# Making h for two batches at once in 64x32 tiles: one fused AdaLN/FFN kernel on Trainium2

## The reference, cut to what matters

```
# x: (8, 512, 2048); each batch b has its own adapter itok[b], rank 16
Bx    = einsum('bni,bri->bnr', x, cond_B[itok])      # 8 x 512 x 16
y     = einsum('bnr,bor->bno', Bx, cond_A[itok])     # never formed
base  = einsum('bsi,oi->bso', y, base_w) + base_b
res   = einsum('bsi,ri->bsr', y, ffn_A)              # 64 wide
p     = softmax(einsum('bsi,ei->bse', y, router_w))  # 16 experts
comb  = top-2 of p, normalised to sum 1, as a dense (b, s, 16)
delta = einsum('bse,bsr,eor->bso', comb, res, ffn_B)
out   = x + base + 0.5 * delta
```

## Time and profile before

| | |
|---|---|
| median of 3 runs | 458.0 us (456.47 to 458.59) |
| profiled execution | 457.73 us, of it the span of the trace 455.9 us |
| PE busy | 412.8 us, 91% |
| DVE busy | 312.6 us, 69% |
| ACT busy | 107.5 us, 24% |
| POOL busy | 40.4 us, 9% |
| DMA | 135.31 MB, mean 297 GB/s |
| mean granted TensorE clock | 0.992 of full |

### The profile page before, as it was taken

One profiled execution on the slowest core, in us unless ns is written; L12 is line 12 of the kernel. 1 busy time (PEld: TensorE's weight loads), 2 busy tenths in 40 slices (PEclk: granted clock), 3 DMA queues, 4 the chain that ended last, 5 costly groups with the idle time before them and its releaser, 6 DMA issues.

```text
span 455.9 us, 6139 instructions
## 1 busy us (share of the span) xinstructions
PE 412.8 (91%) x2240; PEld 275.2 (60%) x2240; DVE 312.6 (69%) x702; ACT 107.5 (24%) x163; POOL 40.4 (9%) x53
## 2 busy tenths in 40 slices
PE   0587998699888999999999999999999999999996
PEld 0466886466555675566556556655675566566675
DVE  3699799968447657766767775677667766757353
ACT  0002025244553240132023102401220132123110
POOL 4020000001100120012002101200120012002000
PEclk9998999999999999999999999999999999999999
DMA  8999999999999997999889888989998998555845
GB/s 228 363 337 335 340 377 345 336 235 352 269 318 256 346 326 265 289 344 309 286 287 384 323 271 282 365 266 291 330 329 287 290 359 313 188 196 197 312 160 186
DMA packets 89360, 135.31 MB, mean 297 GB/s; under 512 B 5506, under 2 KB 43442, under 8 KB 89330
## 3 DMA queue, kind: packets, MB, share of 16 engines
q1 hardware_dynamic: 63168, 102.08, 67.3%
q10 hardware_dynamic: 26162, 32.84, 23.9%
HBM read 99.23 MB, written 35.65 MB: 296 GB/s over the span
## 4 chain that ended last, share of the span: by engine, by line
PE 69%; DVE 13%; DMA 9%; ACTq 3%; ACT 3%; issue 2%; DVEq 0%
PE ps L874 13%; PE ps L895 12%; PE ps L896 10%; PE ps L897 10%; PE ps L908 7%; PE ps L898 5%; DMA xbuf<-in_L_ffn_base_w 5%; DMA early_u<-in_L_ffn_B 5%; PE ps L839 4%; PE ps L829 4%; DVE xT L707 3%; DVE h_r L688 3%; DVE early L640 3%; ACT bexpT L476 2%; ACTq L281 2%
## 5 line engine op out<-in xcount | busy, mean ns | idle before, releaser
L817 DVE TENSOR_TENSOR xbuf<-ps,xbuf 128x512 f32<-128x512 f32 x128 | 87.0, 679 | 109.9 <-PE ps L898 109.8
L895 PE MATMUL ps<-h_r,u_r 128*128 128x512 f32 x256 | 109.3, 427 | 7.1 <-DVE xbuf L817 7.1
L896 PE MATMUL ps<-h_r,u_r 128*128 128x512 f32 x256 | 100.2, 392 | 0.0
L897 PE MATMUL ps<-h_r,u_r 128*128 128x512 f32 x256 | 100.1, 391 | 0.0
L839 PE MATMUL ps<-early 128*128 128x256 f32 x256 | 65.4, 408 | 20.3 <-DVE early L640 20.3
L895 PEld LDWEIGHTS ps<-h_r,u_r 128*128 128x128 f32 x256 | 48.0, 188 | 47.6 <-issue 20.1
L707 DVE STREAM_TRANSPOSE xT<-xbuf 128x512 f32<-128x512 f32 x112 | 72.0, 681 | 0.0
L640 DVE STREAM_TRANSPOSE early<-xbuf 128x256 f32<-128x256 f32 x128 | 65.9, 584 | 5.2 <-issue 3.7
L839 PEld LDWEIGHTS ps<-early 128*128 128x128 f32 x256 | 49.4, 203 | 32.5 <-issue 16.0
L874 PE MATMUL ps<-bexpT,cur 128*32 128x512 f32 x512 | 61.6, 598 | 2.2 <-DVE h_r L688 1.5
L476 ACT ACTIVATE h_r<-ps 128x512 fp32r<-128x512 f32 x64 | 35.7, 594 | 86.6 <-issue 53.8
(11 more groups left out here) (67 smaller groups left out, 206.3 us busy)
## 6 DMA issues: line engine op xcount, KB each, us to landing
out<-xbuf SPq DMA_DIRECT2D x31, 1024.0 KB, 7.1
xbuf<-in_x SPq DMA_DIRECT2D x28, 1024.0 KB, 7.1
xbuf<-in_x ACTq DMA_DIRECT2D x32, 512.0 KB, 9.6
xbuf<-in_x SPq DMA_DIRECT2D x32, 512.0 KB, 8.5
xbuf<-in_L_ffn_base_w SPq DMA_DIRECT2D x16, 512.0 KB, 18.8
xbuf<-in_L_ffn_base_w ACTq DMA_DIRECT2D x16, 512.0 KB, 19.5
gm_r<-g_hilo SPq DMA_DIRECT2D x128, 32.0 KB, 6.4
early_u<-in_L_ffn_B SPq DMA_DIRECT2D x10, 256.0 KB, 17.3
```

What stands on the lines that cost most here:

```text
L817: dve.tensor_tensor(xs, ps[:, ACC + t % 2, :], xs, ALU.add).then_inc(s_out, 1)
L895: pe.matmul(acc, u_r[:, b.q, 0, h, tok_t], hi, start=(h == 0), stop=False)
L896: pe.matmul(acc, u_r[:, b.q, 0, h, tok_t], lo, start=False, stop=False)
L897: pe.matmul(acc, u_r[:, b.q, 1, h, tok_t], hi, start=False, stop=False)
```

## The change

Batches are grouped as 0, (1, 2), (3, 4), (5, 6), 7. A unit is one chunk c of one batch (four tiles); within a pair the units alternate: chunk 0 of both batches, chunk 1 of both, and so on.

h is made per group in rounds (h_round). One round is eight matmuls in tiles of 64 rows by 32 columns: the upper and lower 64 rows (one expert each) go to two PSUM banks, HB and HB+1, and the 32 weight columns are two batches x 16 (a new table, pairs; for a single batch the other 16 are another batch's or zero). For each batch ACT copies bank HB times a 0/1 mask into a new buffer hm (h_masked) and DVE adds bank HB+1 times the other mask (h_merge). h_hi then rounds from hm on ACT, and the low part of h is subtracted on POOL (h_lo); the low part of u moves from POOL to DVE (u_lo). In a pair the two rounds of a chunk stand before tiles 1 and 3 of the first batch's unit, in a single batch before tiles 0 and 1.

The fronts are placed anew (fronts_at): beside the 16 tiles of batch 0 the fronts of batches 1 and 2, two steps per tile; beside the pair (1, 2) those of 3 and 4; beside (3, 4) those of 5 and 6; beside (5, 6) that of 7, one step for every two tiles; beside batch 7 none. From tile 8 on, tiles use four PSUM banks in place of two. tmp, sbx_r and the loads of g are doubled or rearranged for pairs; cur is gone. The order of the experts in the odd place of a pair is swapped to match.

```diff
+        members = [(0,)] + [(b, b + 1) for b in range(1, NB - 1, 2)] + [(NB - 1,)]
+        units, firsts = [], []
+        for group, batches in enumerate(members):
+            firsts.append(len(units))
+            for c in range(OC):
+                for b in batches:
+                    units.append(Unit(len(units), group, c, b))
+        firsts.append(len(units))
...
+        def rounds_at(u):
+
+            i = h_sets.index((u.group, u.c)) + 1
+            pair = len(members[u.group]) == 2
+            if i == len(h_sets) or pair and u.b != members[u.group][0]:
+                return {}
+            return {1: (i, 0), 3: (i, 1)} if pair else {0: (i, 0), 1: (i, 1)}
+
+        def split_at(u):
+
+            return 0 if len(members[u.group]) == 2 else 1
+
+        def fronts_at(u, t):
+
+            m = (u.index - firsts[u.group]) * NT + t
+            if u.group == 0:
+                f, ms = 1 + m // 8, (m % 8 * 2, m % 8 * 2 + 1)
+            elif u.group == NG - 2:
+                f, ms = NB - 1, (m // 2,) if m % 2 == 0 else ()
+            elif u.group == NG - 1:
+                return []
+            else:
+                f, ms = 2 * u.group + 1 + m // MT, (m % MT,)
+            return [(Front(f), k) for k in ms]
...
-        H_AFTER = 122
+        H_AFTER = (114, 124)
+        HT_AT, HM_AT = 118, 120
...
+        XQUAD_AT = {0: ((1, 0), (1, 1)), 2: ((2, 0), (2, 1))}
+        for group in range(1, NG - 2):
+            for i, at in enumerate((0, 1, 4, 5)):
+                XQUAD_AT[firsts[group] + at] = ((2 * group + 1 + i // 2, i % 2),)
...
+        U_AT = {firsts[b // 2]: b for b in range(2, NB, 2)}
+        U_AT.update({firsts[b // 2 + 1] - 1: b for b in range(3, NB, 2)})
...
+        def tile_bank(n):
+
+            return (ACC, ACC + 1)[n % 2] if n < WIDE_FROM else (ACC, ACC + 1, EB, EB + 1)[n % 4]
...
+            def unit(u):
+                for f, g in XQUAD_AT.get(u.index, ()):
+                    xquad_free(sp, Front(f), g)
+                    load_xquad(sp, f + 1, g, range(0, NQ // 2))
+                cols = slice(u.c * BANK, (u.c + 1) * BANK)
+                slot = slice(u.slot * BANK, (u.slot + 1) * BANK)
+                if u.index == len(units) - 1:
+                    for t in range(NT):
+                        sp.wait_ge(s_out, u.index * NT + t + 1)
+                        sp.dma_start(out_v[u.b, :, t, cols], xres[:, t, slot]).then_inc(s_store[u.slot], 16)
+                    return
+                sp.wait_ge(s_out, (u.index + 1) * NT)
+                sp.dma_start(out_v[u.b, :, :, cols], xres[:, :, slot]).then_inc(s_store[u.slot], 16)
+                if u.b == members[u.group][-1] and u.group + 1 < NG:
+                    load_gm(u.group + 1, u.c)
+                if u.index > 0 and u.index + NC - 1 < len(units):
+                    reload(units[u.index - 1], units[u.index + NC - 1])
+
+            def reload(done, new):
...
+            def h_lo(index):
+
                 for h in range(2):
-                    pool.wait_ge(s_uhi, f.n * 2 + h + 1)
-                    pool.tensor_tensor(u_r[:, f.q, 1, h, :], tmp[:, h, :], f32(u_r[:, f.q, 0, h, :]),
-                                       ALU.subtract).then_inc(s_ulo, 1)
+                    pool.wait_ge(s_hhi, 2 * index + h + 1)
+                    pool.tensor_tensor(h_r[:, index % 2, 1, h, :], hm[:, index % 2, h, :],
+                                       f32(h_r[:, index % 2, 0, h, :]), ALU.subtract).then_inc(s_hlo, 1)
+                pool.wait_ge(s_hlo, 2 * index + 2)
...
-            def h_hi(b, c):
+            def h_masked(i, h):
+
+                group, c = h_sets[i]
+                act.wait_ge(s_h, 2 * i + h + 1)
+                for place in range(len(members[group])):
+                    index = firsts[group] + c * len(members[group]) + place
+                    need(act, s_hlo, 2 * (index - 2) + h + 1 if index > 1 else 0)
+                    act.activation(hm[:, index % 2, h, :], ps[:, HB, :], ACT.Copy,
+                                   scale=mask[:, place:place + 1])\
+                       .then_inc(s_ht, 1)
...
+            def h_hi(index):
+
+                u = units[index]
+                i = h_sets.index((u.group, u.c))
+                count = len(members[u.group])
                 for h in range(2):
-                    act.wait_ge(s_h, (b.n * OC + c) * 2 + h + 1)
+                    act.wait_ge(s_hm, merges[i] + h * count + members[u.group].index(u.b) + 1)
                     if h == 0:
-                        need(act, s_acc, (b.n * OC + c - 1) * NT)
-                    copy(h_r[:, c % 2, 0, h, :], ps[:, HB + h, :]).then_inc(s_hhi, 1)
+                        need(act, s_acc, (index - 1) * NT)
+                    copy(h_r[:, index % 2, 0, h, :], hm[:, index % 2, h, :]).then_inc(s_hhi, 1)
+
+            def u_hi(f, h):
+
+                act.wait_ge(s_up, f.n * 2 + h + 1)
+                copy(u_r[:, f.q, 0, h, :], tmp[:, f.q, h, :]).then_inc(s_uhi, 1)
...
+                    if t == 0 and u.index in U_AT:
+                        act.wait_ge(s_acc, tiles_before(u.index))
+                        for h in range(2):
+                            u_hi(Front(U_AT[u.index]), h)
+                    if t in rounds:
+                        h_masked(*rounds[t])
+                    if t == split_at(u) and u.index + 1 < len(units):
+                        h_hi(u.index + 1)
+                    if u.index * NT + t in E_LATE:
+                        copy_experts(E_LATE[u.index * NT + t])
+                    for f, m in fronts_at(u, t):
+                        slot(f, m)
...
-            def h_lo(b, c):
+            def h_merge(i, h):
+
+                group, c = h_sets[i]
+                count = len(members[group])
+                for place in range(count):
+                    index = firsts[group] + c * count + place
+                    dve.wait_ge(s_ht, merges[i] + h * count + place + 1)
+                    dve.scalar_tensor_tensor(out=hm[:, index % 2, h, :], in0=ps[:, HB + 1, :],
+                                             scalar=mask[:, 1 - place:2 - place], in1=hm[:, index % 2, h, :], op0=ALU.mult,
+                                             op1=ALU.add).then_inc(s_hm, 1)
+
+            def u_lo(f):
+
                 for h in range(2):
-                    dve.wait_ge(s_hhi, (b.n * OC + c) * 2 + h + 1)
-                    dve.tensor_tensor(h_r[:, c % 2, 1, h, :], ps[:, HB + h, :], f32(h_r[:, c % 2, 0, h, :]),
-                                      ALU.subtract).then_inc(s_hlo, 1)
+                    dve.wait_ge(s_uhi, f.n * 2 + h + 1)
+                    dve.tensor_tensor(u_r[:, f.q, 1, h, :], tmp[:, f.q, h, :], f32(u_r[:, f.q, 0, h, :]),
+                                      ALU.subtract).then_inc(s_ulo, 1)
...
+                    if u.index in U_AT and t == (0 if U_AT[u.index] % 2 == 0 else 1):
+                        u_lo(Front(U_AT[u.index]))
+                    if t in rounds:
+                        h_merge(*rounds[t])
+                    dve.wait_ge(s_acc, n + 1)
...
-            def h_products(b, c):
-                pe.wait_ge(s_cur, b.n + 1)
-                if b.n == 0:
+            def h_round(i, h):
+
+                group, c = h_sets[i]
+                if i == 0:
+                    pe.wait_ge(s_table, 7)
+                if group == 0:
                     pe.wait_ge(s_ec, PER_C * (c + 1))
-                for h in range(2):
-
-                    need(pe, s_hlo, (b.n * OC + c - 1) * 2 + h + 1)
+                need(pe, s_hm, merges[i] + h * len(members[group]))
+                for q in range(2):
+                    rows = slice(q * R, (q + 1) * R)
                     for j in range(4):
-                        ins = pe.matmul(ps[32 * j:32 * j + 32, HB + h, :], cur[:, b.q, 0:2 * RK],
-                                        bexpT[:, c, 4 * h + j, :], start=True, stop=True)
-                    ins.then_inc(s_h, 1)
-
-            def tile_products(b, c, t):
-                m = c * NT + t
-                acc = ps[:, ACC + t % 2, :]
-                if b.n == 0 and m == 0:
+                        ins = pe.matmul(ps[32 * j:32 * j + 32, HB + q, :],
+                                        pairs[rows, 2 * group:2 * group + 2, :].rearrange("r b k -> r (b k)"),
+                                        bexpT[rows, c, 4 * h + j, :], start=True, stop=True)
+                ins.then_inc(s_h, 1)
...
+                for t in range(NT):
+                    if t in rounds:
+                        h_round(*rounds[t])
+                    for f, m in fronts_at(u, t):
+                        bx_products(f, m)
+                    tile_products(u, t)
+                    if u.index * NT + t in E_LATE:
+                        expert_flips(E_LATE[u.index * NT + t])
+                    for f, m in fronts_at(u, t):
+                        slot(f, m)
```

(44 more changed lines are left out.)

250 lines of the change are left out of this document (125 added, 125 removed).

## The result

The changed kernel takes 486.87 us (median of 4, 485.29 to 490.62) where the kernel before takes 457.61 in the same series: a ratio of 1.0652, 95% interval 1.0583 to 1.0721 (the quotient of the two medians is 1.0639). The forecast was 467, range 449 to 485; the sign was right and the size three times too small. The profiled execution took 485.93 us, its span is 484.0.

The account below looks back on a forecast made before the run. It took DVE and its latency to bound the two chunks with transposes per batch, PE the rest. First tile 118.4 + batch 0 74.0 + two pairs 168.2 + (5,6) 67.5 + batch 7 36.5 + 1.8 = 466.4, said as 467; range 449 to 485.

Parts of the forecast that it names:

- A round takes 1.20 us if eight tiles run at once: PE's h round: two waves, 0.86, plus 0.34 for going there and back, 1.20 us in all.
- Rival D: h rounds: slower, the row halves take turns at 2.06 us a round; 493 us in all, chance 0.09.
- The merge priced as the add: DVE's merges of h: 0.6 us each, like the add, with up to twice that for the range.
- Rival E: DVE's merges: slower, each costs 1.2 us; 485 us in all, chance 0.07.
- Batch 0, 74.0 forecast: Batch 0 pays for the second front beside it: 74.0 us against 47.95 before.
- Rival A: Batch 0: faster, the second front fits under it, 57 us there and 449 in all; chance 0.12.
- the clock as a risk: Batch 0: if PE's long waits lower its granted clock, it comes out later still; no size given.
- Units with transposes in the pairs: Pairs (1,2) and (3,4): chunks with transposes have two lengths, 12.5 and 10.1 us, since PE waits for DVE's transposes.
- Rival B: Pairs (1,2) and (3,4): faster, they run at PE's pace, 74.6 us each; 448 in all, chance 0.06.
- ACT and POOL have room: Per batch and chunk, ACT's two more masked copies (0.6 us each) and POOL's two subtractions (1.3) fit in.
- First tile at 118.4: End of the first stage: POOL does the first h behind u's low half, so 118.4 us instead of 117.97.
- Four banks change nothing in the pairs: First two units of pairs (1,2), (3,4): four banks don't help, as PE waits for transposes; 22.7 us, before 22.8.

Follow-up runs that it names:

- e3: The changed kernel with the two combk transposes and u products moved from steps 13 and 14 to 14 and 15; 470.48 us, ratio 1.0271.
- e10: The changed kernel without the 16 transposes of x for batch 2's front, the second one beside batch 0; 481.33 us in one execution.
- e2: The changed kernel with POOL's subtractions of h (odd units) and sbx delayed, so POOL idles during DVE's routing; 476.75 us, ratio 1.0401.
- e6: The changed kernel with the first h round at step 110 (was 114), masked copy at 112 (118), merge at 122 (120); 483.21 us.
- e5: The changed kernel with two PSUM banks for the tiles all through; 486.75 us, ratio 1.0635.
- e1: The changed kernel with DVE making each step's front transposes before it waits for the tile and adds it; 475.2 us, ratio 1.0351.
- e4: The changed kernel with every round of h making its eight matmuls twice into the same banks; 511.57 us.

## Why the prediction was wrong

- **A round takes 1.20 us if eight tiles run at once: right.** 16 matmuls in 1.09; a unit of four tiles is 8.9 us with two rounds and 6.4 without, so 1.25 for each; (5,6), where PE alone sets the pace, came out at 67.8 for 67.5. Rival D is out.
- **The merge priced as the add: slightly low.** 740 ns (L792), where the add took 679 and the subtraction that it replaces 674 (L817 and L688 before); the masked copy 686 for 594. Rival E is out.
- **Batch 0, 74.0 forecast, 75.6 measured: right in the sum, and partly by luck.** Rival A is out. The waits for combk in it are 3.41 and 4.91 where I had 3.3 and 4.7. e3 and e10 show that these waits and the transposes are two of its parts; a run that takes the whole second front away wasn't made, so their full split stays open. PE's granted clock there is 0.92: I had named the clock as a risk and put nothing for it into the sum, and it costs the 3.9 us behind the two waits. The sum holds because other terms were too long by some 2 us: the first two units are 38.1 us, clock included, for 39.4, the last two 37.7 for 34.6. In e3 the clock of batch 0 is 1.00; of the 9.5 us that it is shorter there, an estimate from these numbers is 1.6 for the first wait, 3.9 for the clock, and the rest for the second wait, which has moved behind its end.
- **Units with transposes in the pairs: right.** 12.5 and 10.1 to the next tile's start stood in the forecast, 12.7 to 13.3 and 10.2 came out; first to third unit are 8.8 to 9.8, 10.4 to 10.7 and 14.5, where its own steps give 8.8, 10.1 and 14.4. Rival B, the pairs at PE's pace, is out.
- **"ACT and POOL have room": the step that failed.** I priced POOL's subtractions of h by POOL's own time. They fall on the routing, where DVE's small instructions wait for POOL, so the wait for combk that I had as 1.4 became 2.6 to 3.4, 6.4 us more in the four fronts; and behind it came 2.9 us of lower clock in (1,2), for which the sum had no term. With 1.3 of small differences the fourth units are 10.1 to 12.2 for 8.6. That is 10.6 of the 13.3 us in the pairs, and e2 took 9.9 of it away by moving POOL's work, the clock's part with it. Why the clock fell in (1,2) and not in (3,4), behind waits of the same length, stays open. "SBUF — State Buffer" of the Trainium skill, section Who interferes with whom, says that a DVE instruction with two SBUF inputs contends with a GpSimd instruction that reads SBUF, and that a cast can contend too, and that whoever comes first keeps the port for its whole instruction. The trace agrees: the stretched instructions are of these kinds and end with POOL's, while the adds, whose one input lies in PSUM, have the same mean as before (681 and 679 ns). Before the change POOL worked beside DVE too, but less: from 166 to 335 us the same three instructions have means of 226, 166 and 142 ns.
- **"First tile at 118.4": failed by 4.1.** I looked at the end of the chain (POOL behind u's low half) and not at where the merge stands in DVE's list of weight transposes. e6 put it right; some 1 to 2.5 us are the execution's own.
- **Four banks change nothing in the pairs: right** (e5).

## What to carry to other kernels

Work moved to an idle engine isn't free when it shares something with a busy one: look at which short instructions of the busy engine it will lie beside, above all in a latency chain. Before an engine's product is halved, find out what the stretch waits for: here the saving of h showed only in (5,6), where the transposes come at half the pace. Try the order inside the waiting engine's list first; moving transposes ahead of adds that nobody waited for was a change of a few lines. And when a stretch grows, compare the waits and the granted clock before it is put down to waiting: in e1 and e4 the waits were as before or shorter, and the clock behind them made the difference.

## What the runs showed of the hardware

- A DVE cast of 128x8 took 142 ns with POOL idle and up to 1.07 us beside a POOL subtraction of 128x512, a TENSOR_TENSOR of 128x8 168 ns and up to 1.18 us (842 ns on the mean), one of 128x512 with both inputs in SBUF 0.68 and up to 1.78 us; STREAM_TRANSPOSE (681 and 682 ns) and the adds from PSUM (679 and 681) kept their times.
- Eight matmuls of 64x32 start in one wave, with 16 weight loads in 0.18 us; a second wave follows, and the 16 end in 1.09. The way there and back costs PE about 0.4 (an estimate: a round's 1.25 less two waves of 0.43), near the 0.34 of the visits with 128x32.
- Behind a wait of 3.4 us for combk the same 23 matmuls took 4.33 us at a granted clock of 1.00, 5.66 at 0.75 and 7.1 at 0.58 (after the change and e1). All four stretches had the same wait before them, so it alone doesn't set the clock.
